# Moving weight preparation, the first q and some gathers around the seam between the two phases of a graph transformer layer

## The chip, the cores and the metric

The kernel runs on one core of one Trainium2 chip. The metric is the time of one execution on the device in microseconds (us), as the median of several runs. TensorE, VectorE, ScalarE, GpSimd and SyncE are PE, DVE, ACT, POOL and SP in the rows of the trace.

## What is computed

12500 nodes of 256 values in float32. The reference, cut to what matters:

```python
xn = layernorm(x)
# graph layer: table of xn @ weight and of attention logits, gathered by src and dst
tmp = einsum('nh,nhd->nd', softmax(leaky_relu(al[src] + al[dst]))[:n], xt[dst[:n]])
# linear attention over all nodes, then a two layer MLP with layer norms
Q, K = elu(xn @ Wq) + 1, elu(xn @ Wk) + 1
KV = einsum('nshd,nshv->nhdv', K, xn @ Wv)          # a sum over ALL nodes
Z = 1 / (einsum('nlhd,nhd->nlh', Q, K.sum(1)) + eps)
m = layernorm((Q, KV, Z combined) @ Wm, g1, b1)
h = relu(concat([xn, m]) @ W1) @ W2
x = x + tmp + xn + layernorm(h, g2, b2)
# mixture of four experts, the best two, and a shared MLP
x = x + shared(layernorm(x)) + gated(experts(layernorm(x)))
```

## The kernel before

The nodes are cut into 25 groups (`NG`): 24 of four tiles of 128 rows and a last one of two tiles of 106. The sum over all nodes splits the kernel into two phases.

**Phase 1** makes per group the normalized rows `xn1`, their transpose (`x1T_hi`, `x1T_lo`), k, the table of the graph layer (`xts`, `als`, stored in DRAM) and adds k times x to `kx` in two banks of PSUM. Matmuls of precision are done as three of a rounded value and a remainder (`_hi`, `_lo`; `split_mm`, L255 to L257). So every operand needs a rounding pass and a subtraction: `xr_hi` (VectorE, L1221), `xr_lo` (GpSimd, L1786), `k_hi` (VectorE, L1232), `k_lo` (GpSimd, L1790). In turn v TensorE does k of group v, the transposes of group v+1, and in two halves the table of group v and `kx` of group v-1. ScalarE does `exp` for k (L919), the rounding of the transposes (L912), the table copies (L929, L930) and the normalization two groups ahead (L894). VectorE does `xr_hi`, the statistics two groups ahead (`bn_stats`, L1190), `kf` (L1226, L1228), `x1T_lo` (L1212, `p1_lowT`) and `k_hi`.

**Weights** are loaded in turns 2 to 17 and rounded in the last turns: ScalarE makes `w_hi` in `plain_parts` (L956), for W2 with its mean taken off (L949) and for the second half of W1 times g1 (L953); VectorE makes `w_lo` (`second_parts`, L1303; W2 in four chunks L1306; W1 L1333) and, in `small_constants` (L1268 to L1297), masks and means.

**The seam.** Every engine's program is straight code here, in an order written by hand, and semaphores (`S[...]`) link them. After phase 1 TensorE does the bias matmuls of h (`hb_mm`, L602, 16 small ones), q of group 0 (`p2_q`), the last `kx`, then the transposes of `kx` (L616), the denominators of group 0 (`p2_den`, L542), `kv` (L623), half a W1 product, the spreading of 1/den (`p2_expand`, L549) and the product with Wm (L630). VectorE copies `kx` (L1338), makes the features of q (`feature_low` L1314, `feature_high` L1320 with ScalarE's `exp` L962 between), `kden` (L1343), 1/den (`one_over_den`, L1425 to L1433) and `kvT` (L1681).

**Phase 2** begins with `turn0` and `turn1`, written out for groups 0 and 1, then `phase2` for each group. A group's message gets its statistics on VectorE (`message_stats`), `rstd` on GpSimd (L1750 to L1757), is normalized on ScalarE (`row_n`, L894), transposed (L467), and multiplied by W1 and W2. GpSimd also issues the indirect loads of the graph layer (`gathers`, L1814 and L1816, a pair per tile); those of group 0 wait until SyncE has seen all table stores land (`tables`), and the loads of `xT` of group 1 stand behind the same point.

## Time and profile before

| what | us |
|---|---|
| median of 3 runs | 1343.5 (1343.08 to 1343.95) |
| the profiled execution | 1352.19 |
| its span | 1350.4 |
| TensorE busy | 1312.1 |
| VectorE busy | 1094.3 |
| GpSimd busy | 762.7 |
| ScalarE busy | 733.6 |

The profiled execution is a run of its own, 8.7 us above the median of the others. The busy times are of its span. TensorE is busy in nearly all of it; the granted clock of TensorE, which the page gives in slices of the span, is above nine tenths of full speed in every one, and only finer windows show where it is lower.

### The profile page before, as it was taken

The page shows a single profiled execution, that of the slowest core. Times are in us where ns is not written, and L with a number is a line of the kernel's source. Part 1 is how long each engine was busy: PE and PEld are TensorE (multiplying, and loading weights), DVE is VectorE, ACT ScalarE, POOL GpSimd, SP SyncE. Part 2 cuts the span into 40 slices and gives each one's busy share as a digit, 9 for nine tenths or more (in the row PEclk, how much of TensorE's full clock was granted, in tenths as well). Part 3 has the DMA queues.
Part 4 walks back from the last instruction along what each step waited for, and adds up shares of the span by engine and source line. Part 5 has one row for each costly group of instructions (what it writes and reads, how often), then busy time and mean ns, then how long its engine had stood idle before and what let it go on. Part 6 is the DMA issues. An engine that isn't in the chain of part 4 may idle for free.

```text
span 1350.4 us, 26301 instructions
## 1 busy us (share of the span) xinstructions
PE 1312.1 (97%) x8812; PEld 1134.8 (84%) x8812; DVE 1094.3 (81%) x2597; ACT 733.6 (54%) x1332; POOL 762.7 (56%) x815
## 2 busy tenths in 40 slices
PE   6999999788999999999999999999999999999998
PEld 6999999676888888888888888888888888888886
DVE  6867677788888888888888888888888888888875
ACT  4555555344646555555646555555645555555654
POOL 5767766735455564656455564656455564656531
PEclk9999999999999999999999999999999999999999
DMA  6787767422121321222121221222121221222000
GB/s 211 250 275 244 245 208 249 135 56 72 35 70 56 78 70 32 68 65 76 36 68 55 78 70 32 68 65 77 36 68 55 78 70 32 70 64 68 26 17 22
DMA packets 65459, 123.23 MB, mean 91 GB/s; under 512 B 31725, under 2 KB 36176, under 8 KB 65422
## 3 DMA queue, kind: packets, MB, share of 16 engines
q1 hardware_dynamic: 57422, 109.25, 25.1%
q0 software_dynamic: 8000, 13.53, 4.6%
q8 instruction: 19, 0.31, 0.1%
q14 instruction: 18, 0.15, 0.0%
HBM read 70.41 MB, written 52.32 MB: 91 GB/s over the span
## 4 chain that ended last, share of the span: by engine, by line
PE 86%; DVE 4%; issue 3%; ACT 3%; POOL 1%; DVEq 1%; POOLq 1%; ACTq 1%
PE psum L255 25%; PE psum L257 25%; PE psum L256 25%; PE psum L467 5%; PE psum L659 1%; PE psum L708 1%; PE psum L699 1%; PE psum L650 1%; ACT scaleT L982 1%; ACTq L1077 1%; PE psum L718 1%; PE psum L542 1%; ACT relu L1075 1%; DVE gnn L1465 1%; POOL ag L1816 0%
## 5 line engine op out<-in xcount | busy, mean ns | idle before, releaser
L1820 POOL TENSOR_TENSOR h_lo<-relu,h_hi 128x1024 fp32r<-128x1024 f32 (+1 forms) x50 | 118.4, 2368 | 148.5 <-ACT h_hi L977 148.4
L255 PE MATMUL psum<-w_hi,h_hi 128*128 128x256 f32 x588 | 166.5, 283 | 1.0 <-ACT e L988 0.8
L257 PE MATMUL psum<-w_hi,h_lo 128*128 128x256 f32 x588 | 166.0, 282 | 0.0
L256 PE MATMUL psum<-w_lo,h_hi 128*128 128x256 f32 x588 | 165.4, 281 | 0.0
L1820 POOL TENSOR_TENSOR s_lo<-relu,s_hi 128x512 fp32r<-128x512 f32 (+1 forms) x45 | 82.7, 1838 | 121.4 <-ACT s_hi L1078 119.8
L255 PE MATMUL psum<-z_hi,w_hi 128*128 128x512 f32 (+1 forms) x300 | 121.6, 405 | 2.4 <-issue 1.1
L255 PE MATMUL psum<-xT_hi,w_hi 128*128 128x512 f32 (+1 forms) x300 | 119.6, 399 | 0.1
L1814 POOL DMA_INDIRECT xg<-table_xt,idx x100 | 99.3, 993 | 35.5 <-issue 31.6
L976 ACT ACTIVATE relu<-psum,h_bias 128x512 f32<-128x512 f32 (+1 forms) x100 | 67.9, 679 | 94.3 <-issue 81.0
L257 PE MATMUL psum<-xT_hi,w_lo 128*128 128x512 f32 (+1 forms) x300 | 117.2, 391 | 0.0
L257 PE MATMUL psum<-z_hi,w_lo 128*128 128x512 f32 (+1 forms) x300 | 117.0, 390 | 0.0
L256 PE MATMUL psum<-xT_lo,w_hi 128*128 128x512 f32 (+1 forms) x300 | 116.9, 390 | 0.0
L256 PE MATMUL psum<-z_lo,w_hi 128*128 128x512 f32 (+1 forms) x300 | 116.9, 390 | 0.0
L255 PEld LDWEIGHTS psum<-w_hi,h_hi 128*128 128x128 f32 x588 | 110.8, 188 | 2.7 <-ACT e L988 1.0
L1816 POOL DMA_INDIRECT ag<-table_al,idx x100 | 94.9, 949 | 30.5 <-issue 30.5
L256 PEld LDWEIGHTS psum<-w_lo,h_hi 128*128 128x128 f32 x588 | 110.9, 189 | 1.1
L257 PEld LDWEIGHTS psum<-w_hi,h_lo 128*128 128x128 f32 x588 | 110.7, 188 | 0.0
L894 ACT ACTIVATE row_n<-psum,nm_m,rs_m 128x256 f32<-128x256 f32 x98 | 47.4, 563 | 101.8 <-POOL nm_m L1757 101.8
L1449 DVE SCALAR_TENSOR_TENSOR base<-xb,rn,b_bc 128x256 f32<-128x256 f32 x98 | 92.1, 980 | 0.2 <-issue 0.2
L988 ACT ACTIVATE e<-psum,e_bias 128x512 f32<-128x512 f32 (+1 forms) x100 | 67.3, 676 | 38.4 <-PE psum L257 38.0
L1790 POOL TENSOR_TENSOR k_lo<-kf,k_hi 128x1024 fp32r<-128x1024 f32 x25 | 62.9, 2518 | 39.5 <-DVE k_hi L1232 39.5
L255 PE MATMUL psum<-mT_hi,w_hi 128*128 128x512 f32 (+1 forms) x200 | 80.8, 404 | 0.7 <-DVE mT_lo L1598 0.7
(274 smaller groups left out, 4291.6 us busy)
## 6 DMA issues: line engine op xcount, KB each, us to landing
xb<-in_x SPq DMA_DIRECT2D x47, 448.0 KB, 3.8
xT_hi_table<-x1T_hi SPq DMA_DIRECT2D x25, 512.0 KB, 2.8
xT_lo_table<-x1T_lo SPq DMA_DIRECT2D x25, 512.0 KB, 3.6
xT_hi<-xT_hi_table SPq DMA_DIRECT2D x25, 512.0 KB
xT_lo<-xT_lo_table SPq DMA_DIRECT2D x25, 512.0 KB
table_xt<-xts SPq DMA_DIRECT2D x24, 455.0 KB, 3.0
out<-xmid SPq DMA_DIRECT2D x24, 448.0 KB
xb<-in_x SPq DMA_DIRECT2D x47, 64.0 KB, 3.8
```

The costliest lines, as they stand in the source:

```text
L255: pe.matmul(out, wh, xh, start=first, stop=False)
L256: pe.matmul(out, wh, xl, start=False, stop=False)
L257: return pe.matmul(out, wl, xh, start=False, stop=last)
L467: last = pe.transpose(psum[:, b + c, j * R:(j + 1) * R], src[:, j, c * P:(c + 1) * P], ident[0:R, 0:R])
L894: act.activation(out[:, j, :], src(j), ACT.Identity, bias=nm[which][:, j:j + 1], scale=rs[which][:, j:j + 1]).then_inc(S[done], 1)
L976: act.activation(out[:, 0:t * R], colT(b, t=t), ACT.Relu, bias=bias)
L988: act.activation(e1[:, e, 0:t * R], colT(bank, t=t), ACT.Relu, bias=e1_bias[:, e:e + 1]).then_inc(S["e1_relu"], 1)
L1449: last = stt(base[:, j, :], xb[par][:, j, :], rn2[par][:, 0, j:j + 1], b2_bc[:], ALU.mult, ALU.add)
L1790: ptt(k_lo[par][:], kf[par][:], k_hi[par][:], ALU.subtract).then_inc(S["k_split"], 1)
L1814: pool.indirect_dma_start(xg[par][:, j, :], None, table_xt.ap(), bass.IndirectOffsetOnAxis(idx[par][:, 1, j:j + 1], 0)).then_inc(S[f"gath{ ...
L1816: pool.indirect_dma_start(ag[par][:, j, :], None, table_al.ap(), bass.IndirectOffsetOnAxis(idx[par][:, 0, j:j + 1], 0)).then_inc(S[f"gath{ ...
L1820: ptt(out, src, hi, ALU.subtract).then_inc(S[done], 1)
```

## The change

On **TensorE** the last two turns of phase 1 are written out. The bias matmuls of h stand right behind k of group 23 and write to columns 256 to 259 of bank 0, which the last group's transposes leave free. q of group 0 stands right behind k of group 24 and uses banks 0 and 1 in place of 2 and 3; the table of group 24 and `kx` of groups 23 and 24 follow.

On **ScalarE** each rounding of weights comes one turn earlier. On **VectorE** `small_constants` comes two turns earlier, the first part of `w_lo` one turn earlier, the second behind `feature_low` of group 0, the W2 chunks in `turn0` and `turn1` (with a semaphore `w2_lo` that TensorE waits for ahead of W2), and `feature_high` of group 0 ahead of the copy of `kx`; `h_bias` is copied in `p1_lowT` of the last group. On **GpSimd** the last group's subtractions take only its two tiles; the gathers of tiles 0 to 2 of group 1 stand behind the `rstd` of group 0's message, and those of tile 3 in `turn1`, behind `h_lo`. `w2_nmean` lives on beyond phase 1.

```diff
--- before.py
+++ after.py
@@ PE: end of phase 1 @@
-            phase1(NG - 2, (NG - 2) % 2)
-            phase1(NG - 1, (NG - 1) % 2, more=False)
+            v, par = NG - 2, (NG - 2) % 2
+            p1_k(v, par)
             pe.wait_ge(S["w_later"], 16 * LATER_LOADS)
             for o in range(4):
                 for c in range(CK):
-                    last = pe.matmul(psum[:, 0, o:o + 1], wslice(w_raw, "W1", 2 + c, o * P, P), b1_col[:, c:c + 1],
-                                     start=c == 0, stop=c == CK - 1)
+                    last = pe.matmul(psum[:, 0, HB_AT + o:HB_AT + o + 1], wslice(w_raw, "W1", 2 + c, o * P, P),
+                                     b1_col[:, c:c + 1], start=c == 0, stop=c == CK - 1)
             last.then_inc(S["hb_mm"], 1)
+            p1_transpose(NG - 1, 1 - par)
+            for pair in range(2):
+                p1_table(v, par, pair)
+                p1_kx(v - 1, 1 - par, pair)
+            p1_k(NG - 1, 1 - par)
             pe.wait_ge(S["w_lo"], 1)
-            pe.wait_ge(S["kf"], NG)
-            p2_q(0, 0, 2)
+            p2_q(0, 0, 0)
             for pair in range(2):
-                p1_kx(NG - 1, (NG - 1) % 2, pair, last=True)
+                p1_table(NG - 1, 1 - par, pair)
+                p1_kx(v, par, pair)
+            for pair in range(2):
+                p1_kx(NG - 1, 1 - par, pair, last=True)
@@ PE: turn 1 of phase 2 @@
                 p2_m(1)
+                pe.wait_ge(S["w2_lo"], 1)
                 pe.wait_ge(S["h_lo"], 2)
@@ ACT: end of phase 1 @@
-            steps(act, phase1, 2, NG - 3)
+            steps(act, phase1, 2, NG - 4)
             act.wait_ge(S["w_later"], 16 * LATER_LOADS)
-            for v in range(NG - 3, NG):
-                phase1(v, v % 2, more=NG - 1 - v)
-                if v == NG - 2:
+            for v in range(NG - 4, NG):
+                phase1(v, v % 2, more=min(2, NG - 1 - v))
+                if v == NG - 3:
                     act.wait_ge(S["w2_mean"], 1)
...
-                if v == NG - 1:
+                if v == NG - 2:
...
-                lo, hi = plain_parts[v - (NG - 3)]
-                act.activation(w_hi[:, lo:hi], w_raw[:, lo:hi], ACT.Copy).then_inc(S["w_hi"], 1)
+                if v < NG - 1:
+                    lo, hi = plain_parts[v - (NG - 4)]
+                    act.activation(w_hi[:, lo:hi], w_raw[:, lo:hi], ACT.Copy).then_inc(S["w_hi"], 1)
@@ DVE: p1_lowT @@
                 dve.wait_ge(S["x1T_hi"], v + 1)
+                if isinstance(v, int) and v == NG - 1:
+                    dve.wait_ge(S["hb_mm"], 1)
+                    dve.tensor_copy(h_bias[:], psum[:, 0, HB_AT:HB_AT + 4])
@@ DVE: weights and end of phase 1 @@
-            steps(dve, phase1, 2, NG - 3)
+            steps(dve, phase1, 2, NG - 5)
...
-                if n == 1:
-                    for k in range(4):
-                        stt(wslice(w_lo, "W2", k), wslice(w_raw, "W2", k), w2_nmean[:, k:k + 1],
-                            wslice(w_hi, "W2", k), ALU.add, ALU.subtract)
+
+            def second_w2(chunks):
+                for k in chunks:
+                    last = stt(wslice(w_lo, "W2", k), wslice(w_raw, "W2", k), w2_nmean[:, k:k + 1],
+                               wslice(w_hi, "W2", k), ALU.add, ALU.subtract)
+                if 3 in chunks:
+                    last.then_inc(S["w2_lo"], 1)
...
-            for v in range(NG - 3, NG):
-                phase1(v, v % 2, more=NG - 1 - v)
+            for v in range(NG - 5, NG):
+                phase1(v, v % 2, more=min(2, NG - 1 - v))
+                if v == NG - 5:
+                    small_constants()
                 if v == NG - 3:
-                    small_constants()
-                else:
-                    second_parts(v - (NG - 3) - 1)
-
-
-            feature_low(0, 2)
+                    second_parts(0)
+
+            feature_low(0, 0)
+            second_parts(1)
+            feature_high(0, 0)
             dve.wait_ge(S["w_hi"], 3)
...
-            dve.wait_ge(S["hb_mm"], 1)
             dve.memset(kden[:], 0.0)
             dve.wait_ge(S["kx"], NG)
             dve.tensor_copy(kx[:], psum[:, 6:8, 0:KX_W]).then_inc(S["kxs"], 1)
-            feature_high(0, 2)
...
-            dve.tensor_copy(h_bias[:], psum[:, 0, 0:4])
@@ DVE: turn0 and turn1 @@
                 soft_chain_in(0, 0, True, False)
+                second_w2((0, 1))
...
                 second_parts(2)
+                second_w2((2, 3))
                 message_stats(1)
@@ POOL: phase1 @@
-                ptt(xr_lo[par][:, :, 0:C], xn1[par][:], xr_hi[par][:, :, 0:C], ALU.subtract).then_inc(S["x_split"], 1)
+                t = tiles(v)
+                ptt(xr_lo[par][:, 0:t, 0:C], xn1[par][:, 0:t, :], xr_hi[par][:, 0:t, 0:C],
+                    ALU.subtract).then_inc(S["x_split"], 1)
...
-                ptt(k_lo[par][:], kf[par][:], k_hi[par][:], ALU.subtract).then_inc(S["k_split"], 1)
+                ptt(k_lo[par][:, 0:t, :], kf[par][:, 0:t, :], k_hi[par][:, 0:t, :], ALU.subtract).then_inc(S["k_split"], 1)
@@ POOL: turn0 and turn1 @@
                 gathers(0, range(T))
-                pool.wait_ge(S["idx1"], 2 * dma16(1, 1))
-                gathers(1, (0, 1))
                 pool.drain()
                 rstd(LM, "mv_m", 1, "rs_m")
-                gathers(1, (2, 3))
+                pool.wait_ge(S["idx1"], 2 * dma16(1, 1))
+                gathers(1, (0, 1, 2))
                 pool.drain()
...
+                gathers(1, (3,))
+                pool.drain()
                 pool.wait_ge(S["m_norm"], T)
                 rstd(LM, "mv_m", 2, "rs_m")
```

TensorE, from k of group 24 to the last `kx` (`wk` is k, `wx` the table, `xr` and `k` are `kx`, `xT` and `w` are q). Before:

```order
L255 MATMUL psum<-wk_hi,x1T_hi 128x256 [waits s_kf,s_x1T]
...
L255 MATMUL psum<-wx_hi,x1T_hi 128x264 [waits s_xts]
...
L255 MATMUL psum<-xr_hi,k_hi 128x258 [waits s_x_split,s_k_split]
...
L255 MATMUL psum<-wx_hi,x1T_hi 128x264 [waits s_xts]
...
L602 MATMUL psum<-b_col,w_raw 128x1 [waits s_w_later]
...
L255 MATMUL psum<-xT_hi,w_hi 128x512 [waits s_xl0,s_kf,s_w_lo]
...
L255 MATMUL psum<-xr_hi,k_hi 128x258 [waits s_x_split,s_k_split]
...
```

And from k of group 23 in the change:

```order
L256 MATMUL psum<-wk_hi,x1T_hi 128x256 [waits s_kf,s_x1T]
...
L603 MATMUL psum<-b_col,w_raw 128x1 [waits s_w_later]
...
L468 MATMUL psum<-ident,xn_0 128x128 [waits s_xn1,s_x1T]
...
L256 MATMUL psum<-wk_hi,x1T_hi 128x256 [waits s_kf,s_x1T]
...
L256 MATMUL psum<-xT_hi,w_hi 128x512 [waits s_xl0,s_w_lo]
...
L256 MATMUL psum<-wx_hi,x1T_hi 128x264 [waits s_xts]
...
L256 MATMUL psum<-xr_hi,k_hi 128x258 [waits s_x_split,s_k_split]
...
L256 MATMUL psum<-wx_hi,x1T_hi 128x264 [waits s_xts]
...
L256 MATMUL psum<-xr_hi,k_hi 128x258 [waits s_x_split,s_k_split]
```

q and the bias matmuls have left the place behind the last turn; q now stands between k of group 24 and the first use of `k_lo` of group 23.

VectorE at the end of phase 1, up to `kden`. Before:

```order
L1306 SCALAR_TENSOR_TENSOR w_lo<-w_raw,w_nmean,w_hi 128x256 x4
L1314 TENSOR_SCALAR qf<-psum 128x1024 [waits s_q_mm]
L1333 SCALAR_TENSOR_TENSOR w_lo<-w_raw,g_col,w_hi 128x512 [waits s_w_hi]
L1333 SCALAR_TENSOR_TENSOR w_lo<-w_raw,g_col,w_hi 128x512
L1336 MEMSET kden 128x64 [waits s_hb_mm]
L1338 COPY kx<-psum 128x516 [waits s_kx]
L1320 SCALAR_TENSOR_TENSOR qf<-psum,qf 128x1024 [waits s_q_exp]
L1343 TENSOR_SCALAR kden<-head_mask,kx 128x4x4 x2
```

And in the change:

```order
L1330 TENSOR_SCALAR qf<-psum 128x1024 [waits s_q_mm]
L1316 TENSOR_TENSOR w_lo<-w_raw,w_hi 128x1280 [waits s_w_hi]
L1336 SCALAR_TENSOR_TENSOR qf<-psum,qf 128x1024 [waits s_q_exp]
L1350 SCALAR_TENSOR_TENSOR w_lo<-w_raw,g_col,w_hi 128x512 [waits s_w_hi]
L1350 SCALAR_TENSOR_TENSOR w_lo<-w_raw,g_col,w_hi 128x512
L1352 MEMSET kden 128x64
L1354 COPY kx<-psum 128x516 [waits s_kx]
L1358 TENSOR_SCALAR kden<-head_mask,kx 128x4x4 x2
```

The W2 chunks are gone, and `feature_high` (`qf<-psum,qf`) stands ahead of the W1 parts and of the `kx` copy.

VectorE in `turn1`, from the last part of `w_lo` to the statistics of group 1's message. Before:

```order
L1303 TENSOR_TENSOR w_lo<-w_raw,w_hi 128x1280 [waits s_w_hi]
L1190 BN_STATS bn_m<-psum 128x6 [waits s_m_mm,s_rs_m]
L1190 BN_STATS bn_m<-psum 128x6
L1190 BN_STATS bn_m<-psum 128x6 [waits s_m_mm]
L1190 BN_STATS bn_m<-psum 128x6
```

And in the change:

```order
L1316 TENSOR_TENSOR w_lo<-w_raw,w_hi 128x1280 [waits s_w_hi]
L1320 SCALAR_TENSOR_TENSOR w_lo<-w_raw,w_nmean,w_hi 128x256 x2
L1200 BN_STATS bn_m<-psum 128x6 [waits s_m_mm,s_rs_m]
L1200 BN_STATS bn_m<-psum 128x6
L1200 BN_STATS bn_m<-psum 128x6 [waits s_m_mm]
L1200 BN_STATS bn_m<-psum 128x6
```

Two W2 chunks now stand between the two.

## Rows read from the trace of the kernel before

**Rows 1.** The page, busy time of each engine.
```profile
PE 1312.1 (97%) x8812; PEld 1134.8 (84%) x8812; DVE 1094.3 (81%) x2597; ACT 733.6 (54%) x1332; POOL 762.7 (56%) x815
```

**Rows 2.** TensorE's waits, 220 to 400 us: releaser, us in total, times, longest.
```profile
PE psum L467 <- ACT row_z L894: 2.9, 1, 2.9
...
PE psum L255 <- DVE z_lo L1667: 2.3, 1, 2.3
...
PE psum L616 <- issue: 1.9, 1, 1.9
...
PE psum L549 <- DVE rdenT L1433: 1.6, 1, 1.6
...
PE psum L630 <- issue: 1.5, 1, 1.5
...
PE psum L255 <- POOL k_lo L1790: 1.1, 1, 1.1
```

**Rows 3.** Busy us of PE, PEld, DVE, ACT, POOL; granted clock, DMA share, GB/s.
```profile
255.00:260.00 5.00, 2.21 (x23) 1.49 (x23) 3.87 (x9) 1.57 (x2) 3.78 (x5) 0.80 0.34 68
```

**Rows 4.** VectorE's timeline around turns 20 and 21: start, us, line, operation, idle before.
```profile
211.43 0.69 DVE L1232 CAST k_hi<-kf 128x1024 fp32r<-128x1024 f32 x1
...
213.84 1.32 DVE L1221 CAST xr_hi<-xn 128x1024 fp32r<-128x1024 f32 x1 [1.72 <-PE psum L257]
...
219.56 1.22 DVE L1212 TENSOR_TENSOR x1T_lo<-psum,x1T_hi 128x1024 fp32r<-128x1024 f32 x1
```

**Rows 5.** VectorE's timeline, first and last instruction of `small_constants` in turn 22.
```profile
231.17 0.17 DVE L1270 MEMSET head_mask<- 128x128 f32 x1
...
236.86 0.47 DVE L1297 SCALAR_TENSOR_TENSOR out_bias<-ob_hi,third,ob_raw 32x256 fp32r<-32x256 f32 x1
```

**Rows 6.** TensorE's timeline at five places of the seam.
```profile
223.09 0.28 PE L255 MATMUL psum<-wk_hi,x1T_hi 128*128 128x256 f32 x1
...
253.46 0.29 PE L255 MATMUL psum<-xr_hi,k_hi 106*128 106x258 f32 x1
...
254.79 0.28 PE L257 MATMUL psum<-xr_hi,k_lo 106*128 106x258 f32 x1
...
258.52 1.08 PE L542 MATMUL psum<-qf,kden 128*32 128x128 f32 x16 [0.94 <-DVE kden L1343]
...
278.61 0.64 PE L542 MATMUL psum<-qf,kden 128*32 128x128 f32 x16 [1.02 <-DVE qf L1320]
```

**Rows 7.** VectorE's timeline at the end of phase 1.
```profile
254.80 1.44 DVE L1333 SCALAR_TENSOR_TENSOR w_lo<-w_raw,g_col,w_hi 128x512 fp32r<-128x512 f32 x2
...
256.24 0.63 DVE L1338 COPY kx<-psum 128x516 f32<-128x516 f32 x1
...
256.79 1.20 DVE L1320 SCALAR_TENSOR_TENSOR qf<-psum,qf 128x1024 f32<-128x1024 f32 x1
...
258.09 0.38 DVE L1343 TENSOR_SCALAR kden<-head_mask,kx 128x16 f32<-128x16 f32 x2
```

**Rows 8.** ScalarE's timeline at the end of phase 1.
```profile
254.92 1.06 ACT L962 ACTIVATE qf<-qf 128x1024 f32<-128x1024 f32 x1 [4.43 <-DVE qf L1314]
```

**Rows 9.** Source line 1306, `W2` low parts: ns min/median/max, first and last start.
```profile
L1306 DVE SCALAR_TENSOR_TENSOR w_lo<-w_raw,w_nmean,w_hi x4: 472/476/2597, 249.4 to 252.7; 128x256 fp32r<-128x256 f32 x4
```

**Rows 10.** VectorE's timeline in turn 0 of phase 2.
```profile
261.34 0.30 DVE L1425 TENSOR_SCALAR psum<-psum 128x128 f32<-128x128 f32 x1 [2.32 <-remote]
...
269.87 1.29 DVE L1662 TENSOR_TENSOR qf<-qf,psum 128x512 f32<-128x512 f32 x2 [3.06 <-remote]
```

**Rows 11.** Timelines of VectorE, GpSimd and ScalarE in turn 1 of phase 2.
```profile
283.11 1.23 DVE L1699 TENSOR_TENSOR mT_lo<-psum,mT_hi 128x1024 fp32r<-128x1024 f32 x1 [0.38 <-issue]
...
292.35 1.48 DVE L1303 TENSOR_TENSOR w_lo<-w_raw,w_hi 128x1280 fp32r<-128x1280 f32 x1
...
293.29 2.78 POOL L1820 TENSOR_TENSOR h_lo<-relu,h_hi 128x1024 fp32r<-128x1024 f32 x1 [2.01 <-ACT h_hi L977]
...
300.12 1.93 ACT L894 ACTIVATE row_n<-psum,nm_m,rs_m 128x256 f32<-128x256 f32 x4 [6.91 <-POOL nm_m L1757]
```

3 lines of the change are left out of this document (2 added, 1 removed), and 2 rows, old and new, of the table SEMAPHORES.

## Prediction

> **What bounds the kernel now.** I read the page first. TensorE is busy 97% of the span [rows 1], and from the second group of phase 2 on it has no idle time worth naming, so time can only be won at the start, at the seam between the two phases and at the end. The change touches the seam, about 213 to 316 us. Next I read what TensorE waited for [rows 2]: 2.9 us for `row_z`, 2.3 us for `z_lo`, 1.9 us before the transposes of `kx`, 1.6 us for `rdenT`, 1.5 us for `kvT`, 1.1 us for `k_lo`, and a few smaller ones. Then I read the granted clock [rows 3]: 0.80 on average from 255 to 260 us, so part of this stretch ran at 1.2 and not 2.4 GHz; TensorE had idled 1.9 us and done four transposes just before. Last I followed VectorE, ScalarE and GpSimd through the timeline of the seam, because every one of these waits is for a chain on them.
>
> **The change, part by part.** Groups are numbered 0 to 24; "turn v" is the stretch of phase 1 in which TensorE makes the k of group v.
>
> *Constants two turns earlier.* `small_constants` takes VectorE from 231.17 to 237.33, 6.2 us [rows 5]. Before, this lay in turn 22, when no more statistics are due for the group after next. Now it lies in turn 20, and turn 21 still has four `bn_stats`. VectorE ended `k_hi` of turn 20 at 212.12 and began `xr_hi` at 213.84 [rows 4]; now it begins at 218.3, 4.5 us later. It gets back 0.6 us, because that cast took 1.32 us where another of the same shape took 0.69 [rows 4] (GpSimd was still at `k_lo`), and half a microsecond of idle time before `kf`. So `x1T_lo` of group 22 ends 3.4 us later than 220.78, at 224.2. TensorE wants it at 223.09, the first matmul of k of group 22 [rows 6]. A new stall of **+1.1 us**. Before the change the slack at that place was 2.3 us and nothing waited. In turns 22 to 24 VectorE catches up: between `k_hi` and the next `xr_hi` alone it idles 1.7 us a turn [rows 4].
>
> *q of group 0 behind the last k.* The 24 matmuls are the same (12 of them take about 3 us either side, and the 16 of `h_bias` 1.8 us); only their place changes. Between the last k and the first use of `k_lo` of group 23 there are now 3 us of work, so the wait of 1.1 us for `k_lo` [rows 2] goes: **-1.1 us**. The last matmul of phase 1 ended at 254.79 + 0.28 = 255.07 [rows 6] and with -1.1 and +1.1 it ends there again.
>
> *What ends last behind it.* The copy of `kx` started at 256.24, behind two `W1` low parts of together 1.44 us [rows 7]. Now `feature_high` of q stands ahead of these. It needs ScalarE's `exp` (1.06 us [rows 8]), and ScalarE does that only behind the last table copies, since these stand ahead in its order. The last table matmul now ends two k-times-x groups before the end; such a group is 12 matmuls, 1.45 us [rows 6], so at about 252.1. Copies 0.5, `exp` 1.06, `feature_high` 1.20, `W1` parts 1.44 and hand-overs bring the `kx` copy to 256.4: not earlier than before, and TensorE idles 2 us there again. The four `W2` low parts that left this place bring nothing by themselves; their time is filled by the wait for ScalarE. But behind the copy, `kden` no longer waits for `feature_high` (1.20 us [rows 7]). It is ready at 257.5, TensorE ends its transposes at 257.75, and `p2_den` starts then and not at 258.52 [rows 6]: **-0.8 us**.
>
> *Clock.* `p2_den` took 1.08 us here and 0.64 us at 278.61 [rows 6]. The 0.9 us of idle time ahead of it is gone, so I take the clock to stay up through it: **-0.4 us**. Bounds: 0, if it falls all the same, and for what a higher clock would give beyond this group see the first rival. The matmuls of `kv` are hidden under VectorE's 1/den, for whose `rdenT` TensorE waited 1.6 us [rows 2].
>
> *`W2` low parts in turns 0 and 1 of phase 2.* One part of 128x256 costs 0.4 us free and 2.6 us when GpSimd has the operands' port (median 472 ns, longest 2597 [rows 9]). Two stand behind the softmax of group 0, ahead of 1/den of group 1 and `mT_lo`. VectorE idled 0.38 us before `mT_lo` at 283.11, which ended at 284.34 [rows 11], and TensorE started on it 0.2 us later. 0.8 - 0.38 - 0.2 gives 0.2 to 0.3: **+0.3 us**. The other two follow the third part of `w_lo`, 292.35 to 293.83, and GpSimd's `h_lo` was issued meanwhile, at 293.29, and ran to 296.07 [rows 11]. I take it that the first `W2` part waits for it, so they end at 296.9. TensorE started the W2 matmuls right behind that `h_lo`, at 296.2, and now waits for `w2_lo` until 296.9: **+0.7 us**. The bounds are 0 (both fit into VectorE's idle time before 295.1) and 2.6 + 0.4 us counted from 293.83, which gives the same 296.9. The Trainium skill, page "SBUF — State Buffer", section "Who interferes with whom", says that a VectorE instruction with two SBUF inputs and a GpSimd instruction that reads SBUF exclude each other and that issue order decides. By that rule it is the 0.7; without it the sum would be 0.7 smaller. The 2597 ns agree with it.
>
> *Gathers.* Before, the indirect loads of tiles 0 and 1 of group 1 stood ahead of the `rstd` of group 0's message, but they were issued by 267.7 and the statistics came at 277.4, so taking them away gives nothing. Ahead of the `rstd` of group 1 there is now one tile's pair, about 2.5 us, from 296.4 to 298.9, where `rstd` began at 297.8. `row_n` of group 1 (300.12, 1.93 us long [rows 11]) comes 1.1 us later, at 301.2 to 303.1. TensorE reaches these transposes at 302.8 already because of the 0.7 above, and ends them 0.1 later or not at all: **0**, bounds 0 and +0.8. The statistics on VectorE, delayed by the same `W2` parts, reach the same moment. The table stores and the gathers of group 0 come some 4.5 us later, as the last table matmul does; they have 9 us of slack before VectorE's softmax.
>
> *GpSimd's halved last tiles* (2 of 4) shorten `k_lo` of group 24, on which nothing waits.
>
> Sum: +1.1 - 1.1 - 0.8 - 0.4 + 0.3 + 0.7 = **-0.2 us**. The profiled execution took 1352.19 us with a span of 1350.4, 8.7 us above the median 1343.5 of the three runs. I put the difference on the median: 1343.3. Bounds of the terms give -1.5 to +1.3.
>
> **Rivals.**
>
> *The late starts fall away.* VectorE started on `p2_den`'s result at 261.34 although the matmuls ended at 259.60 by the trace, and on that of `p2_expand` at 269.87, 3.1 us after it was free [rows 10]; no releaser is shown for either. If these belong to the slow clock of that stretch and the shorter pause keeps it at 2.4 GHz, TensorE gets back the first 1.7 us, and at most also its waits of 1.5 for `kvT` and 2.3 for `z_lo` [rows 2]. That gives -0.2 - 1.7 to -0.2 - 5.5, say -4: **1339.5**. For it: the pause holding only four transposes shrinks from 3.45 us (255.07 to 258.52) to 2.7. Against it: the last late start comes 8 us after the fall, when the clock was long back; and the profiled run is 8.7 us above the others, so part of these gaps may exist only under the profiler. The Trainium skill, page "TensorE: Matmul & The Clock Gate", section "What's actually happening", says that activity is what releases the throttle; by that rule the denser stretch speaks for this rival. Here the row agrees only in that the fall followed a pause.
>
> *VectorE does not catch up* (slower). The constants in turn 20 push VectorE's casts and scalar operations under GpSimd's subtractions of the same turn. One block costs up to 2.1 us (2597 - 472 ns [rows 9]), and there is a place for one in turn 21 (`kf` under `xr_lo` or `rstd`) and one in turn 22. Each adds in full to the stall at group 22 or 23, since the slack is already used: +1.9 to +4.0, say +3: **1346.3**. It decides from the point where `x1T_lo` of group 22 ends later than about 225.5. For it: I count `kf` of turn 21 as ready only 0.2 us before GpSimd leaves `xr_lo`. Against it: in the old turn 22 VectorE won each such race right after its own cast.
>
> **How the numbers follow.** About 0.2%, 2.7 us, is what a measurement of this kernel can tell from no change. My case has 0.57, its own range being 1342.0 to 1344.8; the late starts 0.27; no catching up 0.16. Nearly all of the second case is beyond 1340.8, but some 0.03 of it stays within; 0.03 of my case may end below if only half of the rival is true. So faster 0.27. Of the third, some 0.02 is within 1346.2: slower 0.14, same 0.59. The range has to take in most of both rivals: 1338.5 to 1346.5.
>
> **What would show it.** A wait of about 1.1 us of TensorE for `x1T_lo` near 223 us (rival two: over 2.5, or a second one near 233). No wait for `k_lo` near 244. Before the `kx` transposes an idle time of about 2 us, with VectorE idle for ScalarE's `exp` ahead of it; if that idle time is under 1 us, my reading of ScalarE's order is wrong. `p2_den` right behind the transposes. A granted clock of 1.00 from 255 to 262 us, and the start of 1/den within 0.3 us of `p2_den`'s end, would be rival one's mark. A `W2` low part of over 2 us near 294, and TensorE waiting for it.

## The result, and the profile after

The changed kernel takes 1353.5 us (median of 6 runs, 1349.6 to 1356.7) where the kernel before takes 1344.3 (6 runs, 1343.1 to 1347.0): ratio 1.0067, 95% interval 1.0052 to 1.0082. It is slower by 9 us. The forecast was 1343.3 with a range of 1338.5 to 1346.5, so the result lies outside it.

The two profiled executions differ by much less: 1354.6 us (span 1352.8) against 1352.2 (span 1350.4). The trace of the changed kernel is one of its usual executions; the trace of the kernel before is 8.7 us above the median of the three runs taken with it. Most of what follows hangs on that.

TensorE's waits from 220 to 400 us in the changed kernel, against [rows 2] (releaser, us in total, times, longest):

```profile
PE psum L468 <- ACT row_z L903: 2.9, 1, 2.9
PE psum L256 <- ACT e L998: 2.9, 1, 2.9
PE psum L468 <- ACT row_n L903: 2.6, 2, 1.7
PE psum L624 <- DVE kx L1354: 1.8, 1, 1.8
PE psum L256 <- POOL h_lo L1837: 1.5, 1, 1.5
...
PE psum L256 <- DVE x1T_lo L1225: 0.8, 1, 0.8
PE psum L550 <- DVE rdenT L1446: 0.7, 1, 0.7
```

The waits for `z_lo`, `kvT` and `k_lo` are gone. New are one for `h_lo`, a long one for `row_n`, and a longer one for the experts' `e`. TensorE's timeline, against [rows 6]:

```profile
224.14 0.39 PE L256 MATMUL psum<-wk_hi,x1T_hi 128*128 128x256 f32 x1 [0.75 <-DVE x1T_lo L1225]
...
256.63 0.66 PE L624 MATMUL psum<-ident,kx 128*128 128x128 f32 x4 [1.81 <-DVE kx L1354]
257.22 0.65 PE L543 MATMUL psum<-qf,kden 128*32 128x128 f32 x16
...
265.72 0.36 PE L256 MATMUL psum<-g_hi,z_hi 128*128 128x256 f32 x1
...
291.80 0.36 PE L256 MATMUL psum<-w_hi,h_hi 128*128 128x256 f32 x1 [1.53 <-POOL h_lo L1837]
...
299.49 2.06 PE L468 MATMUL psum<-ident,row_n 128*128 128x128 f32 x8 [1.70 <-ACT row_n L903]
```

TensorE is busy for 1319.9 us, 7.8 more than in [rows 1], for the same 8812 matmuls. Up to 265.72, the first matmul of `p2_m` of group 0, everything goes better than forecast: that matmul was at 273.11 in the trace before, 7.4 us later. All of it is lost again by 340 us. Part of that is the clock. Columns as in [rows 3], 5 us each:

```profile
255.00:260.00 5.00, 3.26 (x33) 2.65 (x34) 4.27 (x11) 0.60 (x1) 3.63 (x4) 1.00 0.70 240
...
275.00:280.00 5.00, 5.00 (x20) 3.97 (x19) 4.57 (x16) 0.93 (x2) 3.79 (x4) 0.84 0.37 46
...
300.00:305.00 5.00, 4.98 (x17) 3.73 (x18) 2.36 (x5) 1.83 (x3) 0.89 (x2) 0.66 0.00 0
...
335.00:340.00 5.00, 4.77 (x27) 4.73 (x28) 2.90 (x15) 0.62 (x3) 0.00 (x0) 0.69 0.27 92
```

TensorE runs at 2.4 GHz through `p2_den`, as forecast, but at 1.2 GHz for about 3.4 us from 273, 300, 314 and 335 us. In the trace before, this happened twice in the same stretch (258 and 316).

The other engines between 281 and 301 us (GpSimd, VectorE and ScalarE in one list), against [rows 11]:

```profile
281.94 0.68 ACT L987 ACTIVATE h_hi<-psum,h_bias 128x512 fp32r<-128x512 f32 x1
...
282.04 1.28 DVE L1675 TENSOR_TENSOR qf<-qf,psum 128x512 f32<-128x512 f32 x2
283.43 1.29 DVE L1680 TENSOR_TENSOR z_lo<-qf,z_hi 128x512 fp32r<-128x512 f32 x2
284.64 1.48 DVE L1316 TENSOR_TENSOR w_lo<-w_raw,w_hi 128x1280 fp32r<-128x1280 f32 x1
286.04 0.87 DVE L1320 SCALAR_TENSOR_TENSOR w_lo<-w_raw,w_nmean,w_hi 128x256 fp32r<-128x256 f32 x2
...
286.95 4.70 POOL L1837 TENSOR_TENSOR h_lo<-relu,h_hi 128x1024 fp32r<-128x1024 f32 x2 [7.02 <-ACT h_hi L987]
...
291.54 0.32 DVE L1205 BATCH_NORM_AGGREGATE mv_m<-bn_m 128x2 f32<-128x6 f32 x3 [0.22 <-issue]
...
293.07 1.20 POOL L1833 DMA_INDIRECT ag<-table_al,idx  x1 [0.30 <-issue]
295.92 1.15 POOL L1765 TENSOR_TENSOR veps_m<-mv_m,eps 128x4 f32<-128x4 f32 x1 [1.66 <-issue]
...
298.87 1.93 ACT L903 ACTIVATE row_n<-psum,nm_m,rs_m 128x256 f32<-128x256 f32 x4 [12.56 <-POOL nm_m L1772]
```

Two things are to be read here. First, GpSimd had the input of its first `h_lo` at 282.6 (the second `h_hi` started at 281.94 and took 0.68), but began at 286.95, right after VectorE's last `W2` part ended at 286.91. VectorE did not wait for GpSimd, as the forecast had it; here GpSimd waited through a whole row of VectorE's instructions. Second, the statistics `mv_m` of group 1 were there at 291.9, but the `rstd` on them began at 295.92: GpSimd issued the gathers of the last tile, to 294.27, and its drain took another 1.66 us.

### The profile page after: what moved, and what is told of

Same layout as the page of the kernel before. It is cut to its first block, busy times and chain, and to the rows that moved or that the text cites. A ratio compares the mean times of both kernels' runs of the same rounds, so it can differ in the third digit from the quotient of the medians.

```text
span 1352.8 us, 26287 instructions
## 1 busy us (share of the span) xinstructions
PE 1319.9 (98%) x8812; PEld 1139.8 (84%) x8812; DVE 1093.8 (81%) x2597; ACT 733.9 (54%) x1332; POOL 760.5 (56%) x815
## 4 chain that ended last, share of the span: by engine, by line
PE 89%; DVE 5%; ACT 2%; issue 1%; DVEq 1%; POOLq 1%; POOL 1%; DMA 0%; SPq 0%; ACTq 0%
PE psum L256 26%; PE psum L257 25%; PE psum L258 25%; PE psum L468 5%; PE psum L667 3%; PE psum L716 1%; PE psum L658 1%; PE psum L550 1%; PE psum L726 1%; PE psum L543 1%; DVE gnn L1478 1%; DMA xb<-in_x 0%; POOLq L1769 0%; POOL h_lo L1837 0%; DVE kf L1241 0%
## 5 line engine op out<-in xcount | busy, mean ns | idle before, releaser
L1807 POOL TENSOR_TENSOR k_lo<-kf,k_hi 128x1024 fp32r<-128x1024 f32 (+1 forms) x25 | 61.0, 2439 | 40.1 <-DVE k_hi L1245 40.1
```

Source lines behind the costliest of these rows:

```text
L1807: ptt(k_lo[par][:, 0:t, :], kf[par][:, 0:t, :], k_hi[par][:, 0:t, :], ALU.subtract).then_inc(S["k_split"], 1)
```

## Experiments

The theories. **G**: the gathers and the drain ahead of the `rstd` of group 1 cost some 4 us, 1.7 of waiting and 2.2 of the low clock behind it. **W**: the `W2` low parts in turns 0 and 1 cost most. **P**: the new end of phase 1 costs it, unseen in the pair of traces. **C**, added after the first group of runs: part of the difference belongs to the kernel before, whose trace has late starts that its median does not have. **A**, added after the second group: the place of the buffers in SBUF. Each run is compared with runs of the kernel before on the same chip. Those took 1353.5 us in the first group of runs, 1344.2 in the second, 1351.2 in the third, 1350.6 in the fourth and 1344.2 in the fifth, so ratios of one group can be set side by side, and those of different groups only with care. The record gives the third and the fifth group the same chip number (7), so the difference of 7 us between these two does not go by that number. The microseconds named in the expectations of the first group assume a kernel before of 1344, which it was not there; what can be read are the differences within the group. The changed kernel itself was not run in it.

### First group (kernel before 1353.5 us): one part undone or done at a time

**Gathers back** (`a_gath_old`):

```diff
             def turn0():
...
                 gathers(0, range(T))
+                pool.wait_ge(S["idx1"], 2 * dma16(1, 1))
+                gathers(1, (0, 1))
                 pool.drain()
                 rstd(LM, "mv_m", 1, "rs_m")
-                pool.wait_ge(S["idx1"], 2 * dma16(1, 1))
-                gathers(1, (0, 1, 2))
+                gathers(1, (2, 3))
                 pool.drain()
...
-                gathers(1, (3,))
-                pool.drain()
                 pool.wait_ge(S["m_norm"], T)
```

> The changed kernel with GpSimd's gathers of group 1 back in their old places (two tiles ahead of the rstd of group 0's message, two behind, none in turn 1). Theory G: the last tile's gathers and the drain ahead of the rstd of group 1 made row_n late by 3.8 us, cost TensorE 1.7 us of waiting and then 2.2 us at the lower clock. Then the wait for row_n near 299 us and the fall of the clock at 300 are gone and the time is 1349.5, some 4 us under the changed kernel (1353.5). Theory W (the W2 low parts of turns 0 and 1 keep GpSimd from h_lo, and that cost most of the 9 us): the wait for h_lo near 290 stays and the time stays at 1352 or above. Theory P (the end of phase 1 itself costs the 9 us, hidden in the profiled pair): 1353, no change.

Measured: 1354.4 us, ratio 1.0006 (0.9997 to 1.0015). The 1349.5 of G did not come.

**Only the gathers new** (`b_gath_new`): the same lines with + and - exchanged, in the kernel before.

> The kernel before with only GpSimd's gathers in the new places. Theory G: about 4 us slower than before, 1348; a wait of over 1.5 us for row_n of group 1. Theories W and P: within 1 us of before, 1344.5, since neither the W2 parts nor the end of phase 1 differ.

Measured: 1356.8 us, ratio 1.0022 (1.0012 to 1.0032). The wait for `row_n` (1.74 us) came as G says, and the kernel is 3.3 us slower than before; the time of 1348 did not come.

**W2 parts back** (`a_w2_old`):

```diff
             second_parts(1)
+            second_w2(range(4))
             feature_high(0, 0)
...
                 soft_chain_in(0, 0, True, False)
-                second_w2((0, 1))
...
                 second_parts(2)
-                second_w2((2, 3))
```

> The changed kernel with the four W2 low parts back at the end of phase 1 (in VectorE's wait for exp of q), none in turns 0 and 1. Theory G: only the last 0.9 us of GpSimd's late start on h_lo goes; 1352.5. Theory W: GpSimd starts h_lo up to 0.9 us or more earlier, the wait of 1.5 us for it goes, with it a fall of the clock; under 1350. Theory P: 1353.5.

Measured: 1356.0 us, ratio 1.0018 (1.0009 to 1.0027). Neither W's 1350 nor G's 1352.5 came.

**Both back** (`a_both_old`).

> The changed kernel with the gathers and the W2 low parts both back: what is left is the end of phase 1 (q behind the last k, weights and constants in other turns). Theories G and W: close to the kernel before, 1344 to 1347 (my prediction for this part alone was -1.2 us). Theory P: 1351 or more, since all of the loss is in what is left.

Measured: 1354.0 us, ratio 1.0003 (0.9994 to 1.0012). None of the expected times came in the sense that was meant: 1354 is above the 1351 of P, but the kernel before took 1353.5 here. By the ratio, what is left of the change costs nothing in this group, which speaks against P; `a_end_only` below, which also has the old addresses, decides it. W has little for it here, 1.0006 with the parts in turns 0 and 1 and 1.0003 without. But G's 4 us did not show as such either. The trace of `a_both_old` says why, here VectorE's and GpSimd's timelines:

```profile
269.55 0.94 POOL L1832 DMA_INDIRECT ag<-table_al,idx  x1 [0.30 <-issue]
...
270.65 1.23 DVE L1330 TENSOR_SCALAR qf<-psum 128x1024 f32<-128x1024 f32 x1 [4.74 <-remote]
...
272.84 1.42 DVE L1200 BATCH_NORM_STATS2 bn_m<-psum 128x6 f32<-128x256 f32 x4 [0.97 <-remote]
```

VectorE starts 4.7 us late and then 1.0 us late, with no releaser on any engine, as in [rows 10]. The first of the two ends 0.2 us after GpSimd has issued the last gather that stands ahead of the `rstd`. Where only the eight gathers of group 0 stand there, this is absent (`a_w2_old`) or there is one late start, of 2.4 us (`b_gath_new`). So in this group the old place of the gathers has late starts at 270 us and the new one the waits at 295, and the two costs offset each other in part. What is left is that the new place is slower by 2.1 us (`a_w2_old` against `a_both_old`) and by 3.3 us (`b_gath_new` against the kernel before); how large each of the two is alone was not measured here.

### Second group (kernel before 1344.2 us)

**The changed kernel again** (`after_again`).

> The changed kernel unaltered, on a chip on which the kernel before took 1353.5 us, as its profiled execution of the first measurement did (1352.2), and not 1343.5. Theory G (the gathers in turn 1 and what follows them): the two parts of the change that were undone one by one gave 1.0018 (W2 parts back) and 1.0006 (gathers back), both 1.0003, so the whole change gives 1.002, 1356. Theory C (the first ratio of 1.0067 comes from stalls that the kernel before had in only some executions): also near 1.002 here, and the kernel before would be at 1344 only where no row of its trace shows a late start without a releaser. If the ratio is again 1.0067, 1362, parts of the change act only together, and both theories are wrong.

Measured: 1355.2 us, ratio 1.0077 (1.0059 to 1.0095). The changed kernel takes nearly what it took in the first comparison; the kernel before is 9 us faster than in the first group. The expectation took this chip for one where the kernel before is at 1353.5. Its third case, a ratio of 1.0067 or more, came by the ratio and not by the time of 1362: what moved is the kernel before.

**All gathers of group 1 behind the first rstd** (`a_gath_all`):

```diff
                 rstd(LM, "mv_m", 1, "rs_m")
                 pool.wait_ge(S["idx1"], 2 * dma16(1, 1))
-                gathers(1, (0, 1, 2))
+                gathers(1, range(T))
                 pool.drain()
...
-                gathers(1, (3,))
-                pool.drain()
                 pool.wait_ge(S["m_norm"], T)
```

> The changed kernel with all four gathers of group 1 behind the rstd of group 0's message, and none ahead of the rstd of group 1. Theory G: no wait of 1.7 us for row_n of group 1 and no fall of the clock at 300 us, and still no late start of VectorE near 270 (its 4.7 us appeared wherever two tiles stood ahead of that rstd again): 3 to 4 us under the changed kernel on the same chip. Rival (the late starts of VectorE follow any gathers that are issued while it crosses into new code): a late start of over 2 us appears near 283, and the time stays.

Measured: 1351.0 us, 4.2 under `after_again`, as G said. `rstd` now follows the statistics, and TensorE's transposes of `row_n` follow its matmuls (timelines of GpSimd and TensorE; the last two rows are of `after_third`, a later trace of the changed kernel):

```profile
292.79 0.28 POOL L1765 TENSOR_TENSOR veps_m<-mv_m,eps 128x4 f32<-128x4 f32 x1 [0.74 <-DVE mv_m L1205]
...
298.04 1.03 PE L468 MATMUL psum<-ident,row_n 128*128 128x128 f32 x8
...
300.33 1.81 PE L468 MATMUL psum<-ident,row_n 128*128 128x128 f32 x8 [1.70 <-ACT row_n L903]
...
313.46 2.17 PE L468 MATMUL psum<-ident,row_z 128*128 128x128 f32 x8 [2.89 <-ACT row_z L903]
```

The eight transposes take 1.03 us where the changed kernel needed 2.06, and the clock no longer falls there. Most of that difference is not the clock. In `after_third` the wait is the same 1.70 us and the clock stays at 2.4 GHz, and the transposes still take 1.81 us, about as long as ScalarE takes for the four tiles of `row_n` that they read (1.93 us).

**The same in the kernel before** (`b_gath_all`).

> The kernel before with the same placement of the gathers. Theory G: no late starts at 266 and 270 us, no late row_n: 1350 or less where the kernel before takes 1353.5. Rival: as before, within 1 us.

Measured: 1346.8 us, ratio 1.0016 (1.0006 to 1.0025). The expectation named a kernel before of 1353.5, which it is not here. Without late starts to remove, eight gathers behind the `rstd` cost 2.6 us: they keep GpSimd to 285.3, `h_lo` begins at 287.6, and TensorE waits 1.3 us for it.

**W2 parts back too** (`a_gath_all_w2`).

> As a_gath_all, with the four W2 low parts back at the end of phase 1 too. If the W2 parts in turn 1 cost anything (GpSimd's h_lo starts late behind them), this is 1 us or more under a_gath_all; if they are hidden, within 0.5 us.

Measured: 1349.4 us, 1.6 under `a_gath_all`. GpSimd begins `h_lo` at 285.72 instead of 287.01, and TensorE waits 0.7 us instead of 1.1.

What is left is 5.2 us over the kernel before. The turns show where. The row of the transposes of `row_z` stands once in every turn; from 364.38 to 1233.05 there are 20 turns of the changed kernel, 43.43 us each (`after_again`):

```profile
364.38 1.03 PE L468 MATMUL psum<-ident,row_z 128*128 128x128 f32 x8
...
1233.05 1.04 PE L468 MATMUL psum<-ident,row_z 128*128 128x128 f32 x8
```

### Third group (kernel before 1351.2 us): 32 bytes

**The changed kernel, 64 bytes** (`a_align`):

```diff
         w2_nmean = sb("w2_nmean", [P, 4])
+        shift = sb("shift", [P, 4])
         s1_bias = sb("s1_bias", [P, 2])
```

> The changed kernel with one unused buffer of 4 floats behind w2_nmean, so that every later buffer lies 64 and not 32 bytes behind its place in the kernel before. Nothing else differs. In the traces so far each turn from group 3 on took 43.43 us in the changed kernel and its variants on the chip where the kernel before takes 1344 us, and 43.22 in b_gath_all; all of it in matmuls whose moving operand is 512 columns of xT, mT, z or s1, which start 1.5 ns later each. These buffers moved by 32 bytes, because w2_nmean now stands ahead of them. Theory A (place in SBUF): turns of 43.22 us and 21 x 0.21 = 4.4 us under the changed kernel. Rival (the turn's length comes from the code or from the order of the loads): turns of 43.43 us, no difference.

Measured: 1346.7 us, ratio 0.9981 (0.9969 to 0.9994); turns of (1225.12 - 359.73) / 20 = 43.27 us. The median hides two sorts of executions: eight took 1345.6 to 1346.9 and four 1350.9 to 1352.1.

The trace, one of the eight, also differs at the seam, where no instruction was changed:

```profile
283.97 2.40 POOL L1838 TENSOR_TENSOR h_lo<-relu,h_hi 128x1024 fp32r<-128x1024 f32 x1 [3.38 <-ACT h_hi L988]
284.10 3.42 DVE L1681 TENSOR_TENSOR z_lo<-qf,z_hi 128x512 fp32r<-128x512 f32 x2
...
287.44 3.68 DVE L1317 TENSOR_TENSOR w_lo<-w_raw,w_hi 128x1280 fp32r<-128x1280 f32 x1
...
291.96 0.39 PE L257 MATMUL psum<-w_hi,h_hi 128*128 128x256 f32 x1 [1.34 <-DVE w_lo L1321]
...
298.27 1.81 PE L469 MATMUL psum<-ident,row_n 128*128 128x128 f32 x8 [0.39 <-ACT row_n L904]
```

The clock did not fall near 273 us, GpSimd got its `h_lo` in ahead of VectorE's `z_lo`, and VectorE waited for GpSimd: its `z_lo` took 3.42 us and not 1.29, its `w_lo` 3.68 and not 1.48. TensorE then waited 1.34 us for the last `W2` part, as the forecast had it, and only 0.39 us for `row_n`. So the time won by this run is not that of the addresses alone; in the 20 turns it is 20 x (43.43 - 43.27) = 3.2 us.

**The kernel before, 32 bytes** (`b_misalign`):

```diff
         h_bias = sb("h_bias", [P, 4])
+        shift = sb("shift", [P, 4])
         s1_bias = sb("s1_bias", [P, 2])
```

> The kernel before with one unused buffer of 4 floats behind h_bias, 32 bytes, and nothing else. Theory A: turns of 43.43 us or more and 4.4 us slower than before (ratio 1.003). Rival: ratio 1.000.

Measured: 1355.0 us, ratio 1.0028 (1.0017 to 1.0038), where 1.003 was expected. Its turns, (1232.99 - 364.20) / 20 = 43.44 us:

```profile
364.20 1.03 PE L468 MATMUL psum<-ident,row_z 128*128 128x128 f32 x8
...
1232.99 1.03 PE L468 MATMUL psum<-ident,row_z 128*128 128x128 f32 x8
```

An unused buffer of 16 bytes makes this kernel 3.8 us slower, with late starts of together 7.1 us like those of [rows 10] still in its trace. That the place of the buffers costs time is shown. That the multiple of 64 bytes is the reason is not; see the last section.

**Only the new end of phase 1** (`a_end_only`): `a_both_old` with `w2_nmean` declared where it was.

> Only the new end of phase 1 (q behind the last k, constants and weights in other turns): gathers, W2 low parts and w2_nmean are all back where they were, and so are the addresses. My forecast for these parts was -1.2 us. Theory A with G: ratio 0.998 to 1.001, turns as in the kernel before. Theory P (the end of phase 1 costs what is left over of the 9 us): over 1.002.

Measured: 1348.5 us, ratio 0.9980 (0.9971 to 0.9989), 2.7 us under the kernel before. P is out. It has one late start, and TensorE waits behind it (timelines of VectorE and TensorE):

```profile
272.75 1.43 DVE L1200 BATCH_NORM_STATS2 bn_m<-psum 128x6 f32<-128x256 f32 x4 [4.48 <-remote]
...
275.80 1.05 PE L543 MATMUL psum<-qf,kden 128*32 128x128 f32 x16 [5.22 <-DVE qf L1336]
```

**One tile ahead, three behind** (`a_best`):

```diff
-                gathers(1, (0, 1))
+                gathers(1, (0,))
                 pool.drain()
                 rstd(LM, "mv_m", 1, "rs_m")
-                gathers(1, (2, 3))
+                gathers(1, (1, 2, 3))
```

> As a_end_only, but with one tile of group 1 gathered ahead of the rstd of group 0's message and three behind. GpSimd is free by then: it ended the gathers of group 0 at 265.8 us and got the statistics at 270. If GpSimd's issue order is what makes h_lo and row_n late, this has neither wait: 1 us under a_end_only or better, and no late start of VectorE near 270 on a chip that shows them. If it is indifferent, within 0.5 us of a_end_only.

Measured: 1347.3 us, ratio 0.9972 (0.9962 to 0.9983), 1.3 under `a_end_only`. The time came as expected, the way to it did not: there is a late start, and a wait of 1.3 us for `h_lo`. Its late start is 1.8 us long and ends at 268.19; the last of its ten gathers ahead of the `rstd` is issued by 268.48. With eight gathers there are none in the variants of the changed kernel, with ten 1.8 us, with twelve 4.5 to 5.7 us.

### Fourth group (kernel before 1350.6 us)

**The kernel before, for its trace** (`before_again`).

> The kernel before unaltered, for its trace on this chip. Over the chips so far it took 1344.2, 1351.2 and 1353.5 us, and its only trace (1352.2) has three late starts of VectorE without a releaser, of together 7.2 us. Theory C: where its time is near 1344, those late starts are missing from its trace, and where it is near 1352 they are there; the turns from group 3 on are at most 0.2 us shorter. Rival: at 1344 the late starts are there too, and the 8 us come from somewhere else.

Measured: 1351.0 us, ratio 1.0001 (0.9991 to 1.0010). VectorE's late starts are there, at nearly the same places as in [rows 10], together 7.1 us:

```profile
261.22 0.30 DVE L1425 TENSOR_SCALAR psum<-psum 128x128 f32<-128x128 f32 x1 [2.27 <-remote]
...
267.56 0.49 DVE L1681 TENSOR_TENSOR kvT<-psum,head_mask 128x128 f32<-128x128 f32 x2 [3.13 <-remote]
...
269.73 1.28 DVE L1662 TENSOR_TENSOR qf<-qf,psum 128x512 f32<-128x512 f32 x2 [1.69 <-remote]
```

**The changed kernel beside it** (`after_third`).

> The changed kernel unaltered, beside the kernel before. Theory C: its time hardly depends on the chip, 1351 to 1356 (its traces have no late start), so that the ratio is near 1.007 where the kernel before is at 1344 and 1.000 to 1.003 where that is at 1351 or above.

Measured: 1351.1 us, ratio 1.0015 (1.0002 to 1.0027), as C says.

**The changed kernel, 64 bytes, on the same chip** (`a_align_2`).

> The changed kernel with the addresses shifted by 64 instead of 32 bytes. Theory A: 4.4 us under after_third on the same chip, turns of 43.2 to 43.3 us against 43.43.

Measured: 1346.1 us, 5.0 under `after_third`; ratio to the kernel before 0.9974 (0.9963 to 0.9985). Its turns take 43.26 us, those of `after_third` 43.44, which is 3.6 us in 20 turns. The rest lies at the seam, where its trace looks like that of `a_align`.

**Only the end of phase 1, again** (`a_end_only_2`).

> Only the new end of phase 1. If the kernel before has no late starts on this chip, this has none either and takes 1343 to 1344, 1 us under it, as forecast for these parts; if it has them, it has one of some 4.5 us, and is 2 to 3 us under the kernel before.

Measured: 1348.8 us, ratio 0.9985 (0.9976 to 0.9995), with a late start of 4.47 us: the second case of the expectation.

### Fifth group (kernel before 1344.2 us)

**The kernel before once more** (`before_3`).

> The kernel before unaltered once more, for its trace where it takes 1344 us, should this chip be such a one. Theory C: the three late starts of VectorE (2.3, 3.1 and 1.7 us on the chip with 1351 us) are missing there, p2_m of group 0 starts near 267 us and not 274. Where it takes 1351 again they are there again.

Measured: 1346.6 us, ratio 1.0010 (0.9999 to 1.0021); the profiled execution took 1344.4. No start of VectorE is without a releaser in it. TensorE and GpSimd:

```profile
258.56 0.65 PE L542 MATMUL psum<-qf,kden 128*32 128x128 f32 x16 [0.94 <-DVE kden L1343]
...
267.46 0.36 PE L255 MATMUL psum<-g_hi,z_hi 128*128 128x256 f32 x1
...
283.24 2.41 POOL L1820 TENSOR_TENSOR h_lo<-relu,h_hi 128x1024 fp32r<-128x1024 f32 x1 [4.11 <-ACT h_hi L977]
...
290.65 0.28 PE L255 MATMUL psum<-w_hi,h_hi 128*128 128x256 f32 x1
...
296.41 1.03 PE L467 MATMUL psum<-ident,row_n 128*128 128x128 f32 x8
...
358.33 1.03 PE L467 MATMUL psum<-ident,row_z 128*128 128x128 f32 x8
...
1222.56 1.04 PE L467 MATMUL psum<-ident,row_z 128*128 128x128 f32 x8
```

So the kernel before has two ways to run, as C says. Its traces of 1351 and 1352 us have 7 us of late starts, the one of 1344 none, and the trace that the forecast was made from was of the first kind, the three runs that it was set against, by their times, of the second. The late starts are not all of the difference. `before` is 7.8 us longer than `before_3`; 3.9 of it is there by `row_z` of the second turn of phase 2 (362.23 against 358.33), and 3.7 comes from the 20 turns (43.40 against 43.21). In `before_again` it is 4.8 and 1.6 us. Why the turns differ was not found.

**The parts together** (`a_behind`): the end of phase 1 with all `W2` parts, all gathers of group 1 behind the `rstd`, `w2_nmean` declared where it was.

> The new end of phase 1 with all W2 low parts in it, all gathers of group 1 behind the rstd of group 0's message, and the addresses of the kernel before: a_gath_all_w2 (1349.4 where the kernel before takes 1344.2) less the 4.4 us of the addresses: 1345.0, on either kind of chip, since its trace should have no late start. That would be 0.4% under the kernel before at 1351 and 0.05% over it at 1344. Rival: the addresses give less where GpSimd's h_lo is waited for, 1347 or more.

Measured: 1344.7 us, ratio 1.0001 (0.9991 to 1.0010). That is 4.8 us under `a_gath_all_w2`, which differs only in the addresses but was measured in another group. It is 9 us under the changed kernel of the first comparison and the same as the kernel before at its best, although the new end of phase 1 is in it: its trace has a wait of 1.7 us for `h_lo`, which `before_3` has not. No version was faster than that one; where the kernel before has its late starts, `a_best` and `a_align_2` beat it by 0.28% and 0.26%.

### The account

`before_3` and `after_again` are the like pair of traces, both of groups with 1344.2 for the kernel before. TensorE in `after_again`:

```profile
266.28 0.36 PE L256 MATMUL psum<-g_hi,z_hi 128*128 128x256 f32 x1
...
292.44 0.36 PE L256 MATMUL psum<-w_hi,h_hi 128*128 128x256 f32 x1 [1.57 <-POOL h_lo L1837]
...
300.12 2.05 PE L468 MATMUL psum<-ident,row_n 128*128 128x128 f32 x8 [1.70 <-ACT row_n L903]
```

- To `p2_m` of group 0: 267.46 to 266.28, **-1.2 us**, the new end of phase 1.
- From there to `W2`: 23.19 to 26.16 us, **+3.0**. Of it 1.2 is the low clock from 273.9 to 277.3, and 1.6 the wait for `h_lo`.
- `W2` to the transposes of `row_n`: 5.76 to 7.68, **+1.9**, the late `rstd`.
- To the transposes of `row_z` (308.71 and 314.66): 12.30 to 14.54, **+2.2**. In `after_third`, with the same wait and no fall of the clock, this stretch takes 13.13 us, so 0.8 of it belongs to the late `row_n` and 1.4 to the low clock.
- The 20 turns: (1222.56 - 358.33) / 20 = 43.21 to 43.43 us, **+4.4**, the addresses.
- The rest, between and behind these: +0.5.

Before rounding the sum is 10.9 us, the difference of the spans (1342.6 and 1353.5); the medians of the second group differ by 11.0. The runs undo it in the same sizes: 1355.2, less 4.2 for the gathers, less 1.6 for the `W2` parts, less 4.8 for the addresses gives the 1344.7 of `a_behind` within rounding. The size of each step holds for this order of undoing; `a_align` shows that the waits at the seam hang together. With the pair of the first comparison the addresses show less, since the turns of that trace of the kernel before took 43.40 us.

## Why the prediction was wrong, by its own steps

**Constants two turns earlier, +1.1.** Right: a wait of 0.75 us at 224.14, and the place is 1.05 us later. VectorE caught up; the rival would need a second wait, and there is none.

**q behind the last k, -1.1.** Right: no wait for `k_lo`.

**What ends last behind it, -0.8.** Right in kind. The idle time before the `kx` transposes is 1.81 us (2 forecast), ScalarE's `exp` is the reason, and `p2_den` follows the transposes. In the like pair its start moves from 258.56 to 257.37, -1.2.

**Clock, -0.4.** Not borne out. `p2_den` ran in 0.65 us in the first trace of the changed kernel, but also in `before_3`; in `after_again` it took 1.08 us, with the clock low from 256.8 to 260.3. It varies between executions of either kernel. The four terms of phase 1 come to -1.2, which is what the like pair shows, but that the sums agree is partly luck, since the clock term is not in it.

**W2 low parts, +0.3 and +0.7.** The step that failed is "GpSimd's `h_lo` was issued meanwhile ... I take it that the first `W2` part waits for it". In the traces of the first two comparisons it ran the other way. In `before_3` GpSimd starts `h_lo` at 283.24, 0.08 us before VectorE begins its own row of instructions. In the first trace of the changed kernel its input is ready after VectorE has begun (282.62 against 282.04), and it begins only when VectorE stops, at 286.95. Part of the reason is likely the low clock, which made TensorE's h late by 1.2 us. The `W2` parts lengthen VectorE's row by 0.87 us. TensorE waited 1.5 to 1.6 us for `h_lo`, and undoing the parts gave 1.6. In `a_align` and `a_align_2`, the same program with other addresses, it ran as forecast: VectorE waited, and TensorE waited 1.3 and 1.2 us for the last `W2` part. In `after_third` GpSimd got in between the two `W2` parts, which then took 3.01 us together and not 0.87. So what failed is the certainty about who waits, which varies between executions, and the size: 1.2 to 1.6 us and not 0.7. The +0.3 for the two parts in turn 0 was not measured by itself. The Trainium skill, page "SBUF — State Buffer", section "Who interferes with whom", says that issue order decides who blocks, and the traces agree for `z_lo`, `w_lo` and the `W2` parts, all with two SBUF inputs (1.48 us for `w_lo` when it went first, 3.68 behind `h_lo`); by the same page the division `qf<-qf,psum`, with one, should have let GpSimd in at 282.7, which it did not in the first trace of the changed kernel.

**Gathers, 0, bounds 0 to +0.8.** This step failed most. It is "ahead of the `rstd` of group 1 there is now one tile's pair, about 2.5 us, from 296.4 to 298.9, where `rstd` began at 297.8". It placed new work in a schedule that was 6 us late: in `before_3` the statistics are there at 292.1, before the gathers are through. It left out the drain behind them (1.66 us), although the diff shows it, it priced no fall of the clock, and it did not see that a late `h_lo` makes these gathers late too. Measured by `a_gath_all`: 4.2 us, by the like pair 1.9 and 0.8 for the late `row_n` and 1.4 for the clock.

**No term at all: the addresses, +3.6 to +4.4** by the turns of `a_align_2` and of the like pair, 3.8 by `b_misalign`. The text ahead of the forecast says that `w2_nmean` lives on beyond phase 1, and the forecast gave it no term. This is some 40% of the loss, and alone enough to leave the forecast's own range of 1342.0 to 1344.8. (The bounds that the forecast states with its terms give at most -1.2 to +1.0, not its -1.5 to +1.3; neither reaches the result.)

**The rival "late starts fall away" (1339.5).** In the pair of traces it happened in full: p2_m 7.4 us earlier, no late start left. The clock was not the reason: in `after_again` it was low from 256.8 to 260.3, and there is no late start either. It could not bring 1339.5, since the 1343.5 that the sum was put on belong to executions that have no late starts. The forecast saw the 8.7 us and named them as evidence against the rival, but did not draw the consequence for its base: times from the trace and the median were of two different ways of running.

## What to carry over

If the profiled execution is 0.6% above the median of the same kernel, look for what it contains and the others don't before placing new work in its gaps; here 7 us of starts without a releaser made a slot that in the runs of 1344 us doesn't exist. And before an engine is given work ahead of a short step on the way of TensorE (here `rstd`), count its drains, and put into the range that the wait may bring a fall of the clock with it, here 1.4 us behind a wait of 1.7.
